# A gated cross-attention block on one core: where the bias is added, and three groups of work put elsewhere in the order

## The reference

```python
x = x + tanh(g_xattn) * relu(att(layernorm(x), ctx, ctx) @ ffn_w.T + ffn_b)   # relu on q, k and v, softmax over 256 keys
x = x + tanh(g_ffn)  * ffn(layernorm(x))
# ffn: xr, xk = mixes of a row with the row before it; out = sigmoid(xr @ W_r.T) * (relu(xk @ W_k.T)**2 @ W_v.T)
```

## Time and profile before

| | |
|---|---|
| median of three runs | 2935.4 us |
| profiled execution | 2935.97 us |
| its span, first to last instruction | 2934.1 us |
| TensorE busy in matmuls | 2833.1 us, 97% |
| VectorE busy | 2349.9 us, 80% |
| ScalarE busy | 1568.1 us, 53% |
| GpSimd busy | 1044.8 us, 36% |
| DMA engines, mean | 139 GB/s |

### The profile page before, as it was taken

One profiled execution on the slowest core, in us unless ns is written; L12 is line 12 of the kernel. 1 busy time (PEld: TensorE's weight loads), 2 busy tenths in 40 slices (PEclk: granted clock), 3 DMA queues, 4 the chain that ended last, 5 costly groups with the idle time before them and its releaser, 6 DMA issues. The chain is left out here.

```text
span 2934.1 us, 71298 instructions
## 1 busy us (share of the span) xinstructions
PE 2833.1 (97%) x23168; PEld 2183.8 (74%) x23168; DVE 2349.9 (80%) x4175; ACT 1568.1 (53%) x2828; POOL 1044.8 (36%) x902
## 2 busy tenths in 40 slices
PE   3899999999999999999999999999999999999998
PEld 2677777777777777777777777777777777777776
DVE  5788888888888878878878878888888888888874
ACT  4455555555555555555555555555555555555552
POOL 0233333343343333333343333333333333333333
PEclk9999999999999999999999999999999999999999
DMA  5544545535445445445445445445445455355431
GB/s 167 153 129 145 154 121 151 155 121 154 151 123 156 143 127 159 138 130 159 138 131 159 133 138 155 129 145 153 126 147 156 121 152 154 122 154 149 126 104 42
DMA packets 405258, 408.56 MB, mean 139 GB/s; under 512 B 164577, under 2 KB 329441, under 8 KB 405218
## 3 DMA queue, kind: packets, MB, share of 16 engines
q1 hardware_dynamic: 352994, 340.92, 39.7%
q10 hardware_dynamic: 52224, 67.12, 7.0%
HBM read 272.64 MB, written 134.22 MB: 139 GB/s over the span
## 5 line engine op out<-in xcount | busy, mean ns | idle before, releaser
L699 DVE TENSOR_REDUCE m_nat<-bank 128x2 fp32r<-128x512 f32 x1024 | 694.6, 684 | 142.0 <-PE bank L906 141.5
L477 ACT ACTIVATE q_st<-bank 96x512 fp32r<-96x512 f32 x512 | 303.9, 593 | 765.7 <-PE bank L875 765.7
L496 ACT ACTIVATE probs<-bank 128x512 f32<-128x512 f32 x1024 | 593.6, 590 | 195.8 <-PE bank L918 187.2
L718 DVE RECIPROCAL o_val<-bank 128x256 f32<-128x256 f32 x256 | 449.3, 1755 | 60.4 <-PE bank L944 53.2
L918 PE MATMUL bank<-q_st,k_st 97*128 97x256 f32 x2048 | 437.9, 295 | 18.3 <-DMA q_st<-m_t 18.1
L906 PE MATMUL bank<-k_st,q_st 96*128 96x256 f32 x2048 | 430.0, 292 | 6.0 <-DMA k_st<-k_dram 4.5
L918 PEld LDWEIGHTS bank<-q_st,k_st 97*128 97x128 f32 x2048 | 345.5, 190 | 84.5 <-issue 22.6
L906 PEld LDWEIGHTS bank<-k_st,q_st 96*128 96x128 f32 x2048 | 356.8, 192 | 58.1 <-issue 5.9
L364 POOL TENSOR_TENSOR o_lo<-o_mv,o_hi 128x512 fp32r<-128x512 f32 x128 | 174.0, 1360 | 583.3 <-ACT o_hi L503 583.3
L397 POOL TENSOR_TENSOR xm<-xm 128x512 f32<-128x512 f32 x128 | 137.6, 1075 | 637.0 <-ACT xm L540 637.0
L708 DVE CAST m_t<-bank 4x256 fp32r<-4x256 f32 x256 | 105.1, 411 | 286.2 <-PE bank L884 286.1
(11 more groups left out here) (90 smaller groups left out, 5893.6 us busy)
## 6 DMA issues: line engine op xcount, KB each, us to landing
k_st<-k_dram SPq DMA_DIRECT2D x256, 256.0 KB, 3.6
k_raw<-ctx_t_dram SPq DMA_DIRECT2D x256, 128.0 KB, 3.1
x_ln<-x_dram SPq DMA_DIRECT2D x256, 128.0 KB
k_dram<-k_high SPq DMA_DIRECT2D x64, 512.0 KB, 3.0
k_dram<-k_raw SPq DMA_DIRECT2D x64, 512.0 KB, 4.5
k_st<-k_dram SPq DMA_DIRECT2D x256, 128.0 KB, 3.5
o_dram<-o_val SPq DMA_DIRECT2D x256, 128.0 KB, 1.7
o_mv<-o_dram SPq DMA_DIRECT2D x512, 64.0 KB, 2.0
```

Of the source, the lines that this page charges most:

```text
L477: nc.scalar.activation(q_st[0:QK, c, :, P * u:P * u + P], tp_bank[0:QK, :].rearrange("p (g t) -> p g t", g=GR), ACT.Copy).then_inc(q_stack ...
L496: nc.scalar.activation(probs[:, n // GR % 2, n % GR, :, :].rearrange("p v t -> p (v t)"), st_bank[n % 2][:, :], ACT.Exp, scale=SCALE).then ...
L699: nc.vector.tensor_reduce(m_nat[:, c % 2, :, n % GR:n % GR + 1], s_bank[n % 2][:, :].rearrange("p (u y) -> p u y", u=NU), AX_X, ALU.max, n ...
L718: nc.vector.reciprocal(o_val[:, :], pv_bank[:, T:2 * T]).then_inc(rden_ready, 1)
```

## The change

- The bias matmul in `project` goes. A tile b_all holds the bias on all 128 partitions (loaded so by one DMA), and ScalarE copies it into `dense_bank[u]` (`set_bias`) once it has read that bank in `kt_relu`; `project` waits for this and adds onto it with no matmul that opens the sum. The first bank is set after `load_v(i, 1)`, ahead of `q_high(i + 1, 0)`, the second after `q_high(i + 1, 1)`.
- Two matmuls in iteration 1 write both banks once (`banks_marked`), so that later sums without an opening matmul are added. `key` opens only with its first part.
- The bias's low part, its DMA and the wait on it go from the start.
- `values(i - 1, 3)` moves from step 1 to step 0, right behind the first key part; `denominators(i - 1, 3)` behind scores 7; turn 1 stands alone where both were.
- VectorE: `norm_o(i - 1, 3)` ahead of `copy_m(i, 1)`; `k_low(i + 2)` from behind head_max(i + 1, 6) to behind copy_m(i + 1, 0).
- SyncE: `write_k(i + 2)` ahead of `read_o(i, 0)` and `write_o(i, 2)`.

```diff
@@ sync: load_w, iteration
-                    sp.wait_ge(setup_dve, 1)
-                    sp.dma_start(b_rows[1:2, :].bitcast(F32), b_low.bitcast(F32)).then_inc(b_low_moved, 16)
-
-                    sp.wait_ge(b_low_moved, 16)
-                    sp.wait_ge(setup_act, 3)
+                    sp.wait_ge(setup_act, 1)
...
                 load_w(i)
+                write_k(i + 2, par)
                 read_o(i, 0)
                 write_o(i, 2)
-                write_k(i + 2, par)
...
-            sp.dma_start(b_raw, bias.rearrange("(a n) -> a n", a=1)).then_inc(setup_loaded, 16)
+            sp.dma_start(b_all[:, :], bias.rearrange("(a n) -> a n", a=1).broadcast_to([P, D])).then_inc(setup_loaded, 16)
@@ scalar
+            def set_bias(b, u):
+
+                if on(b):
+                    if isinstance(b, int) and b == 0:
+                        act.wait_ge(banks_marked, u + 1)
+                    if on(b - 1):
+                        act.wait_ge(kt_relued, 2 * (b - 1) + u + 1)
+                    nc.scalar.activation(dense_bank[u][:, :], b_all[:, :], ACT.Copy).then_inc(bias_set, 1)
...
                 load_v(i, 1)
+                set_bias(i - 1, 0)
                 q_high(i + 1, 0)
...
                 q_high(i + 1, 1)
+                set_bias(i - 1, 1)
                 o_high(i - 1, 1)
@@ vector: iteration
                 finish(i - 3, 1, 1 - par)
+                norm_o(i - 1, 3)
                 copy_m(i, 1)
-                norm_o(i - 1, 3)
                 mix_r(i - 2)
...
                 copy_m(i + 1, 0)
+                k_low(i + 2)
...
                 head_max(i + 1, 6)
-                k_low(i + 2)
@@ tensor: weights_split, product, project, key, iteration
+                    for u in range(NU):
+
+                        nc.tensor.matmul(dense_bank[u][:, :], ones_r[:, :], w_hi[W_X][:, 0, :],
+                                         start=True, stop=True).then_inc(banks_marked, 1)
...
-                        freed(*users)
-                        nc.tensor.matmul(dense_bank[u][:, :], ones_r[:, :], b_rows[:, :], start=True, stop=False)
+                        pe.wait_ge(bias_set, NU * b + u + 1)
...
-                                     (xk_hi[:, kc, :], xk_lo[:, kc, :]), kc == 0, kc == KC - 1)
+                                     (xk_hi[:, kc, :], xk_lo[:, kc, :]), m == 0 and kc == 0, kc == KC - 1)
...
                 dense(0, 0)
+                values(i - 1, 3)
                 scores(i, 7)
+                denominators(i - 1, 3)
                 dense(0, 1)
 
                 shifted_scores(i, 1)
-                values(i - 1, 3)
                 turn(1)
-                denominators(i - 1, 3)
                 dense(0, 2)
```

More of the change, by code:

```diff
@@ L88, in flamingo_block @@
         th = sb("th", [P, NU, D])
-        b_rows = sb("b_rows", [P, D], F32R)
+        b_all = sb("b_all", [P, D])
         ones_r = sb("ones_r", [P, P], F32R)
@@ L110, in flamingo_block @@
         ident_raw = xn[:, 0, 0:P]
-        b_raw = th[0:1, 0, :]
-        b_low = th[0:1, 1, :].bitcast(F32R)
         bank = [es.enter_context(nc.psum_tensor(f"bank{n}", [P, 512], F32)) for n in range(8)]
@@ L132, in flamingo_block @@
         setup_dve = sem("setup_dve")
-        b_low_moved = sem("b_low_moved")
+        banks_marked = sem("banks_marked")
+        bias_set = sem("bias_set")
         var_ready = sem("var_ready")
@@ L435, in _ @@
             nc.scalar.activation(tg[:, :], gates[:, :], ACT.Tanh).then_inc(setup_act, 1)
-            nc.scalar.activation(b_rows[0:1, :], b_raw, ACT.Copy).then_inc(setup_act, 1)
             def split_high(i, n):
@@ L634, in _ @@
         def _(dve):
-            nc.vector.memset(b_rows[:, :].bitcast(F32), 0.0)
             nc.vector.memset(ones_r[:, :].bitcast(F32), 1.0)
@@ L837, in iteration @@
                 head_max(i + 1, 6)
-                k_low(i + 2)
-            dve.wait_ge(setup_act, 3)
-            nc.vector.tensor_tensor(b_low, b_raw, b_rows[0:1, :].bitcast(F32), ALU.subtract).then_inc(setup_dve, 1)
+            dve.wait_ge(setup_act, 2)
             nc.vector.tensor_scalar(tgh[:, :], tg[:, 1:2], 0.5, None, ALU.mult).then_inc(setup_dve, 1)
-            dve.wait_ge(setup_dve, 2)
+            dve.wait_ge(setup_dve, 1)
             pipeline(dve, iteration)
@@ L854, in weights_split @@
                 if isinstance(i, int) and i == 1:
-                    pe.wait_ge(setup_act, 3)
-                    pe.wait_ge(b_low_moved, 16)
                     pe.wait_ge(w_hi_ready, 8)
                     pe.wait_ge(w_lo_ready, 8)
+                    for u in range(NU):
+                        nc.tensor.matmul(dense_bank[u][:, :], ones_r[:, :], w_hi[W_X][:, 0, :],
+                                         start=True, stop=True).then_inc(banks_marked, 1)
             def freed(*copies):
@@ L950, in product, with project @@
                 for n, (a, c) in enumerate(((0, 0), (1, 0), (0, 1))):
-                    mm = nc.tensor.matmul(dst, lhs[a], rhs[c], start=first and n == 0, stop=last and n == 2)
+                    mm = nc.tensor.matmul(dst, lhs[a], rhs[c], start=first and n == 0, stop=last and n == 2,
+                                          skip_group_check=True)
                 return mm
-            def project(b, u, part, *users):
+            def project(b, u, part):
                 if on(b):
                     if part == 0:
-                        freed(*users)
-                        nc.tensor.matmul(dense_bank[u][:, :], ones_r[:, :], b_rows[:, :], start=True, stop=False)
+                        pe.wait_ge(bias_set, NU * b + u + 1)
                         pe.wait_ge(o_hi_ready, NU * b + u + 1)
@@ L1018, in dense @@
                     elif q < 4:
-                        project(b1, u, part, (kt_relued, b2, 2, u + 1))
+                        project(b1, u, part)
                     elif q < 6:
```

## The result

The changed kernel takes 2979.2 us (median of four runs, 2977.59 to 2979.98) against 2934.57 (four runs, 2933.16 to 2940.07) on the same chip: the ratio is 1.0148, interval 1.013 to 1.0165. It is slower by 44.6 us. Forecast were 2957 and a range of 2908 to 2993, so the rise is twice the forecast one (22).

What follows compares the result with a forecast made beforehand. TensorE, busy 97%, bounds the kernel, but VectorE has no room where groups move. +0.45 us a batch gives +27, start -4, tail -1: together +22, so 2957 us; range for 8 in 10: 2908 to 2993.

Steps and rivals of the forecast that it cites:

- bias of the first half: First bias matmul of `project` on TensorE goes: -0.23 us a batch.
- bias of the second half and its wait: Second bias matmul of `project` and the o_lo wait behind it go: up to -0.95, taken as -0.85 us a batch.
- wait A: New TensorE wait in step 0: last group's values wait for VectorE's norm_o(i-1, 2), 0.68 us a batch.
- term C: TensorE from the moved values to turn 2: values and denominators now parted by matmuls, +0.12 us a batch.
- wait B: New TensorE wait at turn 2 for VectorE's copy_m(i, 1), behind norm_o(i-1, 3): 0.80 us a batch (0.4 to 1.1).
- Setting +0.52 to +0.45: Steady batch sum lowered because late landings partly fall into the new waits; +27 us in place of +32.
- The start: Before the batches: SyncE's 4.4 us wait for the second bias row goes, -4 us (0 to -5).
- write_k ahead of read_o: cost 0, 1.8 of slack: SyncE's queue: first half's read behind the key writes still gives o_lo 1.8 us before norm_o(i-1, 3) needs it; cost 0.
- rival 4: First half's o_mv lands over 1.8 us later than taken, delaying norm_o, copy_m, turn 2: 2994 and more; chance 0.08.
- Rivals 1 and 2: VectorE catches up: only one of A and B there, 2916, chance 0.15; neither there, o wait goes, 2865, chance 0.08.
- Rival 3: Second half's o chain stays late, read 3.0 after write: +0.5 us a batch more, 2987; chance 0.15.
- the old wait: TensorE's wait on o_lo ahead of `project`'s second half, 62 times, 33.7 us before; forecast to go.

Runs made afterwards that it cites:

- run 1: Changed kernel with VectorE taking copy_m(i, 1) ahead of norm_o(i - 1, 3) again; 2964.44 us, ratio 1.0094.
- 2: Changed kernel with TensorE's order of before: the last group's values and denominators in step 1 again; 2994.31 us, ratio 1.0199.
- kernel 4: Changed kernel with TensorE's and VectorE's order of before around the last group; ScalarE's bias, early k_low and write_k stay; 2918.18 us, ratio 0.994.
- run 6: Changed kernel with k_low(i + 2) ahead of copy_m(i + 1, 0) on VectorE; 2954.52 us, ratio 1.0063.
- run 10: Changed kernel with k_low ahead of copy_m(i + 1, 0), copy_m(i, 1) ahead of norm_o(i - 1, 3), read_o(i, 0) ahead of write_k; 2913.85 us, ratio 0.9926.
- run 3: Kernel before with only the bias part (ScalarE writes the bias, shorter start included), all orders as before; 2927.72 us, ratio 0.9971.
- run 5: Changed kernel with SyncE sending read_o(i, 0) ahead of write_k, then write_o(i, 2); 2970.52 us, ratio 1.0122.
- run 9: Run 7 with the bias matmuls of the kernel before, and its longer start, in place of ScalarE's writes; 2884.09 us, ratio 0.9823.
- run 7: Kernel 4 with SyncE's order read_o(i, 0), write_k, write_o(i, 2); 2854.54 us, ratio 0.9722 against the kernel before.
- run 12: Run 7 with write_k last, behind read_o(i, 0) and write_o(i, 2), as in the kernel before; 2923.58 us, ratio 0.9955.
- 11: Run 1 with GpSimd squaring only one column of each row, the rest left unsquared; 2917.25 us, ratio 0.9935.

## Why the prediction was right, and what it missed

The sign and the mechanisms held: both new waits are there 62 times, the old one is gone, VectorE idles by 0.99 ahead of head_max 7, and every run that puts VectorE's or TensorE's order back or gives VectorE room ahead of norm_o (1, 2, 4, 6) takes away the wait that it should. The time was 22 us too low, and with it the rise was forecast at half its size, because terms were too small. By the steps:

| step | taken, us a batch | measured |
|---|---|---|
| bias of the first half | -0.23 | -0.23 |
| bias of the second half and its wait | -0.85 | -0.93 (f) |
| wait A | +0.68 | +0.80 (b, run 6 against after) |
| term C | +0.12 | +0.15 (rest of b and c; 0.14 in run 10) |
| wait B | +0.80 | +0.90 (c, after against run 1) |
| TensorE's spacing behind a wait, other | none | +0.11 |
| sum | +0.52, set to +0.45 | +0.80 |

The measured price of the first line is d in run 3 against before (4.67 and 4.90). The first line went as worked out; in the second, the 0.1 given back for late batches was hardly needed. **Wait B was 0.10 too small**, and the rows say where: from head_max 7 to the copy VectorE takes 4.22 (1571.76 to 1575.98), where the working had 1.98 + 1.79 + 0.34 = 4.11, and x1's sum in it takes 0.86 against 0.75 in its undisturbed place, as GpSimd's o_lo runs at 1572.11 to 1573.40 beside it. Run 5 bears this out: with o_lo early, x1's sum is back at 0.75 and c falls by 0.10. I had taken a duration from a stretch in which GpSimd was not at work beside it. **Wait A was 0.12 too small**: 0.05 of it is VectorE's chain (7.57 from copy_m to norm_o's product, 1562.17 to 1569.74, where I had 6.39 + 1.13), the rest I can't divide. **No price stood for what follows a wait on TensorE**: turn 2 occupies 0.32 here (1576.44 to 1576.76) and 0.25 before, and d is 4.73 in all kernels with wait B or near it (4.75 in run 6) against 4.67 or 4.68 in those without it, runs 1 and 10 with their wait of scores 10 set aside. **Setting +0.52 to +0.45** was wrong by itself: the argument (late landings fall into the new waits) had no row, and it cost 4 us of the 22. *The start* gave 7 and not 4: the bias edit alone moves the end of that wait by 2.9 (54.66 in run 3), and the keys' order alone by 4.8 (52.67 in run 9; the first write of the keys goes out at 10.54 in the changed kernel and at 17.45 before). The working had only the bias.

**"write_k ahead of read_o: cost 0, 1.8 of slack"** is the step that held by luck. The read goes out right behind the keys as taken, but o_high starts 6.5 us behind its first issue, at 1571.40. That is 9.2 behind copy_m's start; the forecast had 7.6 (1539.44 to 1547), so 1.7 of the 1.8 of slack are used up. In the changed kernel this costs 0.10 a batch (c of run 5, by way of x1's sum; 8.7 us in its medians), in every order in which TensorE comes to turn 1 in time 0.93 (runs 2 and 4), and without it the read's landing is hidden (run 7). I had it at 8 in 100 as rival 4; it should have stood as a price on every good version. The Trainium skill ("DMA: Bandwidth & Descriptors", "Issuing engines are not separate DMA queues") has the transfers of all issuing engines interleave on the same 16 engines. No run here separates transfers of two issuing engines: what is shown is one issuer, SyncE, whose read takes 3.43 us to issue behind the megabyte of keys and 1.81 without it. A wait of an engine that is not the bottleneck (ScalarE's on o_mv, 170.3 us in the earlier trace rows and 263.5 after) is nothing to pass over: it told where the next wait would come from.

**Rivals.** Rivals 1 and 2 are excluded, since A and B are both there. Runs 1 and 6 show that A and B are not two prices to be added or taken off one by one. They are one fact, VectorE late in a single stretch; take one off, and a third wait or a longer second one takes 0.73 or 0.36 of its 0.80 to 0.90. Rival 3 (the o chain stays late) is excluded: the second half waits for nothing, as the write-to-read of 1.73 against my 2.2 shows. My belief that the old wait would go was right, but for a part of the change only: it is the early write_k (69 us between run 12 and run 7), and not the early values, since kernel 7 has them late. The bias on ScalarE gives nothing in a steady batch while that wait stands (44.43 in run 3 against 44.37), and 29.5 us, start included, once it is gone (run 9).

So the change is three edits that pay together, 80 us when the read is kept ahead of the keys, and two that cost: the early values, and norm_o ahead of the copy. These two are worth 61 us (the changed kernel against kernel 4) with the read behind the keys; moving the read ahead of the keys then gives the other 64 (kernel 4 against 7), and only 9 while they stand (run 5).

**Left open**: the 0.07 of A's excess that no row explains, 0.04 of the 0.12 in g between kernels 9 and 7, and the rest of the 7.5 us of run 3. norm_o ahead of the copy with the values late and the read early was not run, so the 125 us are not divided further.

## What to carry to other kernels

Ask of every moved piece what the engines do in that very stretch, not in the mean. VectorE was busy for only 80% of the span, but had no room where TensorE's values were moved to, and TensorE paid for it in waits. Repairing one of these waits uncovered the next. Take durations of two-input VectorE instructions by the neighbour on GpSimd that they will have, and not by the row that they have now. Before a large write is put ahead of a small read in one queue, look who waits for the read, also on an engine that is half idle.

## What the runs showed of the hardware

- A VectorE instruction with two inputs in SBUF stretches while GpSimd works on SBUF. mix_r's four take 1.65 us alone and 2.45 beside a square of 1.11; the second x1's sum of a batch 0.75, and 1.19 in the mean of kernel 6; k_low 1.25, and 2.01 in kernel 6, where it stands ahead of copy_m and beside xk_lo on GpSimd. The timelines of kernel 4, first VectorE's, then GpSimd's, show the extreme:

```profile
1319.12 1.85 DVE L775 SCALAR_TENSOR_TENSOR x<-th,tgh,x 128x512 f32<-128x512 f32 x1
...
1319.15 1.27 POOL L358 TENSOR_TENSOR o_lo<-o_mv,o_hi 128x512 fp32r<-128x512 f32 x1 [9.34 <-ACT o_hi L496]
```

  The excess of 1.10 is nearly GpSimd's 1.27. The Trainium skill ("SBUF — State Buffer", "Who interferes with whom") says that a VectorE instruction with two SBUF inputs contends with a GpSimd instruction that reads SBUF, and that reductions do not. Runs 5 and 11 agree on the first. No run tests the second: head_max, a reduction whose input is a PSUM bank, keeps its mean of 682 to 685 ns in every kernel.
- ScalarE's copy of 128x512 from SBUF into a bank takes 603 to 605 ns in the mean, its copies from SBUF to SBUF 624 to 631 in the changed kernel (o_high 631), where the output type differs too (fp32r).
- A read of small pieces behind a megabyte of writes needs 3.43 us to issue, and o_high starts 6.5 after the first issue (1564.89 to 1571.40). With no keys just ahead of it the issue takes 1.81 (the second half's read). The last group's write of 128 KB lands 3.14 after its issue where it is sent 4.5 behind the keys (kernel 12), and 1.71 where it is sent 9.6 behind them (kernel 7); all four are medians.
